# First layer's attention values: nine split products per chunk replaced by full-precision products on halves and quarters of the array

## Chip, cores and metric

The kernel runs on one core of a Trainium2 chip. The metric is the device time of one execution in microseconds (us). The kernel before takes 928.72 us, the median of 3 runs (927.98 to 929.9).

## The reference, cut to what matters

The network is two layers, each an attention onto a context of 154 keys per batch and a feed-forward part. The change touches only the attention of the first layer:

```
x: (2, 1024, 256)   ctx_768: (2, 154, 192)        all float32
q = (layernorm(x) @ Wq)  -> 16 heads of 64
k, v = ctx @ Wk, ctx @ Wv -> 16 heads of 64
attn = softmax(q @ k^T / 8) over the 154 keys of the same batch
x = x + tanh(g_xattn[0]) * ((attn @ v) @ Wo + bo)
```

After it come the first layer's mixture of 8 experts, a second attention (8 heads of 128, all 308 keys) and a coupling network. They are not changed.

## The kernel before

**Work and loops.** The 2048 rows of x are 16 tiles of 128. The attention goes through them two at a time: 8 pairs, in the function `pe_pairs` for TensorE and `dve_pairs`, `act_pairs`, `pool_first` for the other engines. The 16 heads lie in 8 chunks of 128 columns, two heads each; two chunks (four heads) are a group. A pair is worked off in 8 steps, n = 0 to 7. A "row" is what one step makes: the scores of one group (n // 2) for one of the two tiles (n % 2). The 8 pairs are peeled bodies and one hardware loop (pairs 5 and 6), which is the only place where pieces of the experts' weight W2 are split (L1046 on ScalarE in steps 1, 3 and 5, L827 on VectorE in steps 2, 4 and 6).

**Split products.** TensorE's fast float32r product is used with both operands split in a high and a low part, so one product is three matmuls (`pe_split`, L535 to L537). Plain f32 matmuls appear in the trace as two MATMUL records, each with a weight load of its own. The scores (L563) are plain f32: each head has a contraction of 64, and the two heads of a chunk lie on the upper and lower half of the array's rows and write two banks of the accumulator memory (PSUM).

**Order on TensorE.** The order is written out by hand. In step n: scores of row n + 1; transposes of row n - 1 (`pe_pair_probsT`, 5 transposes of 128x128, L573, into banks 4 and 5); a block of 12 split matmuls, which are queries in steps 0, 1, 6, 7 and output products in steps 2 to 5; then `values(n)`. In step 7 the transposes come before the scores. At the end of step 5 the next pair's x is transposed (L542) into bank 7, which must be free: it waits for `y_done`, the VectorE instruction (L834) that reads the output product of step 5 there. Bank 7 also holds the queries and outputs of all steps, so each block waits until the one before has been copied out.

**Values.** A chunk's values product (`pe_pair_pv`) takes three split products of 128x128 by 128x256 (both tiles at once): the 128 whole keys of either head, each with the other head's columns zero (`V0` has zero pads for it), and the remaining 26 keys of four heads, which lie at 32 partitions each in the fifth transposed block. That is 9 matmuls per chunk, 18 per group. The first chunk of a group runs at the end of an odd step, the second at the end of the even step that follows. Both write bank 6.

**The chain around it.** VectorE finds the row maximum (L877) of the scores. ScalarE does four exponentials with sums (L1084). VectorE takes reciprocals (L881), GpSimd multiplies (L1193, L1195) into the single buffer `normed`. After the transposes ScalarE copies them to the high part (L1066) and VectorE subtracts for the low part (L887). After a group's values ScalarE copies bank 6 to the high part of the output operand (L1071) and VectorE makes its low part (L894). ScalarE's and VectorE's queues are first in, first out. ScalarE's order in step n is: L1066 of row n - 1, the exponentials of row n + 1, a query copy (L1058, steps 0, 1, 6, 7) or x copy (L1053, step 5), in even steps L1071, and in the loop a piece of W2. VectorE's is: reciprocals of row n, row maximum of row n + 1, L887, normalising or statistics (L776), `add_y` (L834, steps 3 and 5), x low part (L869, step 5), in even steps L894, and in the loop a piece of W2.

**Before the first pair** the keys and values are computed (`pe_kv`, L427), 8 units for the values. ScalarE copies each to a high part (L474, L477) and VectorE subtracts (L456, L462).

Of the kernel before, what the change touches and what calls it, by code (L numbers as in the profile page):

```python
# [15 lines left out]
F32 = mybir.dt.float32  # L16
F32R = mybir.dt.float32r
U32 = mybir.dt.uint32
ALU = mybir.AluOpType
# [29 lines left out]
def flamingo(nc, t_in, out):  # L49
# [31 lines left out]
    with ExitStack() as ctx:  # L81
# [38 lines left out]
        def split_parts(offset, **shapes):  # L120
            with ExitStack() as place:
                if offset:
# [16 lines left out]
                                     for part in (W2_low, W2_high)]  # L139
        V0_WIDTH = 3 * 64 + P  # L140
        V0_high0, V0_low0 = split_parts(0, V0_high0=[P, NC, V0_WIDTH], V0_low0=[P, NC, V0_WIDTH])
        V0_high1, Wq0_high, xT0_low = split_parts(W2_SIZE, V0_high1=[P, NC, V0_WIDTH], Wq0_high=[P, DK, INNER],
                                                  xT0_low=[P, DK, PAIR])
# [3 lines left out]
        class Region:  # L147
# [20 lines left out]
        V0_low1, = split_parts(V0_AT, V0_low1=[P, NC, V0_WIDTH])  # L168
        P0_AT = V0_AT + NC * V0_WIDTH + 2 * 640 + NC * PAIR
        p0T_high, p0T_low, o0T_high = split_parts(P0_AT, p0T_high=[P, 2, 5, PAIR], p0T_low=[P, 2, 5, PAIR],  # L170
                                                  o0T_high=[P, NC, PAIR])
        V0 = ((V0_high0, V0_low0), (V0_high1, V0_low1))
# [11 lines left out]
        ctx_rows = reg_a.part(3 * DC, "p (r d) -> p r d", r=3)  # L184
        reg_a.at = P0_AT + 20 * PAIR
# [174 lines left out]
        o_ps = banks[:, 6, :]  # L360
        misc_ps = banks[:, 7, :]
# [6 lines left out]
        pT_parts = ((p0T_high, p0T_low), (pT_high, pT_low))  # L368
# [37 lines left out]

        def pe_kv(pe, units):
            pe.wait_ge(sem("wk_in0"), 16)
            for n in units:
# [4 lines left out]
                if n >= (4 if n < NC else NC + 3):  # L414
                    pe.wait_ge(sem("kv_sb"), n - (3 if n < NC else 2))
                    if n < NC:
                        pe.wait_ge(sem("kv_high"), n - 3)
# [28 lines left out]
        def dve_kv(dve, L, units):  # L446
            for n in units:
# [5 lines left out]
                elif kind == "v":  # L453
                    high, low = V0[a]
                    dve.wait_ge(sem("kv_high"), n + 1)
                    last = dve.tensor_tensor(whole_values(low, half), bank.rearrange("p (c i n) -> p c i n", c=4, i=2),  # L456
                                             whole_values(high, half).bitcast(F32), ALU.subtract)
                else:
                    high, low = V0[a]
                    dve.wait_ge(sem("kv_high"), n + 1)  # L460
                    for j in range(4):
                        last = dve.tensor_tensor(rest_values(low, half, j), rest_bank(bank, j),  # L462
                                                 rest_values(high, half, j).bitcast(F32), ALU.subtract)
# [1824 lines left out]
```

## Time and profile before

| | us |
|---|---|
| median of 3 runs (lowest, highest) | 928.72 (927.98, 929.9) |
| the profiled execution, device time | 927.16 |
| its span, first to last instruction | 925.3 |
| TensorE busy | 882.1 (95%) |
| VectorE busy | 563.1 (61%) |
| ScalarE busy | 519.3 (56%) |
| GpSimd busy | 373.7 (40%) |

PE is TensorE's matmuls, PEld its weight loads, DVE VectorE, ACT ScalarE, POOL GpSimd. Matmuls are pipelined: the duration of one is longer than the distance from its start to the next one's. A view that merges neighbours gives the start of the first and the length to the end of the last. The first layer's attention proper lies between about 42 and 300 us of the span.

### The profile page before, as it was taken

Reading aid. Unit: us, or ns where it says so; the run is one execution under the profiler, and the core shown is the slowest. Engines: PE = TensorE matmul, PEld = TensorE weight load, DVE = VectorE, ACT = ScalarE, POOL = GpSimd, SP = SyncE. Lnnn points to the kernel's source line nnn. Section 1 sums busy time; section 2 is a strip of 40 time slices with the busy share of each in tenths; the row PEclk is TensorE's granted clock in tenths of the full one; section 3 lists DMA queues with packets and bytes.
Section 4 is the critical chain, followed back from the end, with each engine's and each line's share of the span. In section 5 each row is a group of like instructions: output and inputs, shape, how many; then the busy total and the mean of one; then the engine's idle time right before and its main releaser. Section 6 shows DMA issues by size and latency. Waiting matters only on the chain.

```text
span 925.3 us, 20373 instructions
## 1 busy us (share of the span) xinstructions
PE 882.1 (95%) x6837; PEld 800.3 (86%) x6838; DVE 563.1 (61%) x1331; ACT 519.3 (56%) x1466; POOL 373.7 (40%) x530
## 2 busy tenths in 40 slices
PE   6989999999999999999999987999999999999996
PEld 4579999998898769999999986999999999987653
DVE  4665565556665774443444447877777776666466
ACT  5676776677775344334443462655655555552565
POOL 3173443444343143545455551534434443443000
PEclk9999999999999899999999997999999999999998
DMA  9000000330001557777777813000000000000002
GB/s 266 3 1 2 1 1 1 123 95 1 0 1 50 168 198 245 265 236 253 253 254 255 241 68 94 24 24 13 12 23 11 12 1 1 2 1 1 1 1 91
DMA packets 36674, 76.19 MB, mean 82 GB/s; under 512 B 4941, under 2 KB 22721, under 8 KB 36481
## 3 DMA queue, kind: packets, MB, share of 16 engines
q1 hardware_dynamic: 32865, 65.11, 21.8%
q0 software_dynamic: 3744, 10.23, 3.3%
q8 instruction: 39, 0.64, 0.3%
q14 instruction: 26, 0.21, 0.1%
HBM read 66.02 MB, written 9.31 MB: 81 GB/s over the span
## 4 chain that ended last, share of the span: by engine, by line
PE 87%; DVE 5%; DMA 3%; ACT 2%; issue 2%; POOL 1%; SPq 0%; DVEq 0%; POOLq 0%
PE banks L535 16%; PE banks L537 15%; PE banks L536 15%; PE banks L1530 14%; PE banks L573 8%; PE banks L563 5%; PE banks L427 3%; PE banks L1815 2%; PE banks L504 1%; PE banks L1826 1%; PE banks L1820 1%; PE banks L1808 1%; DMA region_a<-in_L_ffn_b 1%; PE banks L500 1%; PE banks L542 1%
## 5 line engine op out<-in xcount | busy, mean ns | idle before, releaser
L1084 ACT ACTIVATE region_a<-banks,negmax 128x154 f32<-128x154 f32 (+1 forms) x384 | 161.7, 434 | 29.1 <-DVE negmax L877 27.8
L1530 PE MATMUL banks<-region_b,region_a 128*128 128x128 f32 x1248 | 146.5, 276 | 1.2 <-ACT region_b L1566 1.2
L1530 PEld LDWEIGHTS banks<-region_b,region_a 128*128 128x128 f32 x1248 | 142.7, 192 | 2.1 <-ACT region_b L1566 0.9
L1230 POOL TENSOR_TENSOR region_a<-region_a,recip 128x640 f32<-128x640 f32 x64 | 80.3, 1255 | 136.1 <-DVE recip L881 136.1
L1193 POOL TENSOR_TENSOR region_a<-region_a,recip 128x512 f32<-128x512 f32 x64 | 66.7, 1042 | 138.6 <-DVE recip L881 99.5
L877 DVE TENSOR_REDUCE negmax<-banks 128x4 f32<-128x616 f32 (+1 forms) x128 | 100.5, 785 | 28.8 <-PE banks L563 15.5
L1621 DVE SCALAR_TENSOR_TENSOR region_b<-banks,region_a,region_b 128x128 f32<-128x128 f32 x156 | 43.9, 345 | 106.1 <-PE banks L1530 99.5
L573 PE MATMUL banks<-ident,region_a 128*128 128x128 f32 x640 | 94.0, 277 | 3.9 <-DVE pT_low L887 1.6
L573 PEld LDWEIGHTS banks<-ident,region_a 128*128 128x128 f32 x640 | 72.2, 140 | 14.1 <-issue 9.8
L535 PE MATMUL banks<-xT_high,Wq_high 128*128 128x256 f32 x256 | 78.3, 306 | 2.9 <-DVE xT_low L869 2.0
L1066 ACT CAST pT_high<-banks 128x640 fp32r<-128x640 f32 x64 | 44.4, 694 | 64.1 <-PE banks L573 64.1
L1084 ACT ACTIVATION_READ_ACCUMULATOR region_a<-banks,negmax 128x1 f32 x384 | 78.4, 204 | 0.0
L537 PE MATMUL banks<-xT_high,Wq_low 128*128 128x256 f32 x256 | 72.7, 284 | 0.0
L536 PE MATMUL banks<-xT_low,Wq_high 128*128 128x256 f32 x256 | 72.6, 284 | 0.0
L1066 ACT CAST p0T_high<-banks 128x640 fp32r<-128x640 f32 x64 | 44.6, 698 | 49.5 <-PE banks L573 49.5
L1573 ACT ACTIVATE region_b<-banks,region_a 128x128 f32<-128x128 f32 x156 | 44.6, 369 | 45.6 <-PE banks L1530 45.6
L887 DVE TENSOR_TENSOR p0T_low<-banks,p0T_high 128x640 fp32r<-128x640 f32 x64 | 52.6, 822 | 16.4 <-ACT p0T_high L1066 15.3
L887 DVE TENSOR_TENSOR pT_low<-banks,pT_high 128x640 fp32r<-128x640 f32 x64 | 52.7, 824 | 14.3 <-ACT pT_high L1066 13.1
L535 PE MATMUL banks<-p0T_high,V_high 128*128 128x256 f32 x192 | 54.9, 286 | 1.6 <-DVE o0T_low L894 1.6
L535 PEld LDWEIGHTS banks<-xT_high,Wq_high 128*128 128x128 f32 x256 | 49.0, 191 | 8.4 <-DVE xT_low L869 3.6
L535 PE MATMUL banks<-pT_high,V_high 128*128 128x256 f32 x192 | 54.3, 283 | 1.9 <-DVE oT_low L894 1.9
L1662 POOL COPY home_now<-home 128x1 uint32 (+1 forms) x39 | 20.7, 531 | 84.3 <-DVE region_b L1642 74.6
(294 smaller groups left out, 2542.2 us busy)
## 6 DMA issues: line engine op xcount, KB each, us to landing
region_a<-in_L_ffn_W SPq DMA_DIRECT2D x39, 1024.0 KB
W<-in_L_ffn_W SPq DMA_DIRECT2D x1, 4096.0 KB, 15.1
W<-y_rows SPq DMA_DIRECT2D x16, 256.0 KB, 2.8
out<-x SPq DMA_DIRECT2D x8, 256.0 KB, 2.2
x<-in_x SPq DMA_DIRECT2D x1, 1536.0 KB, 13.3
region_b<-in_L_xattn_Wq SPq DMA_DIRECT2D x1, 1024.0 KB, 9.4
region_b<-in_L_xattn_Wo SPq DMA_DIRECT2D x1, 1024.0 KB, 14.1
xn_rows<-region_b SPq DMA_DIRECT2D x1, 1024.0 KB, 4.8
```

The source lines that it names most:

```text
L535: pe.matmul(o, left[0], right[0], start=start, stop=False)
L536: pe.matmul(o, left[0], right[1], start=False, stop=False)
L537: return pe.matmul(o, left[1], right[0], start=False, stop=stop)
L563: mm = pe.matmul(scores[:, n % 2, i, u * NKEY:(u + 1) * NKEY], q0[half, c, rows], K0[half, b, c, 0:NKEY], start=True, stop=True)
L573: mm = pe.transpose(probsT_ps[:, m * P:(m + 1) * P], row[:, m * P:(m + 1) * P], ident[:])
L877: dve.tensor_reduce(into, source, AX.X, ALU.max, negate=True).then_inc(sem("bias_ready"), 1)
L887: dve.tensor_tensor(low[:, n // 2 % 2, :, at], probsT_ps[:, 0:640].rearrange("p (m n) -> p m n", m=5), high[:, n // 2 % 2, :, at].bitcast( ...
L1066: act.copy(pT_parts[L.index][0][:, n // 2 % 2, :, at], probsT_ps[:, 0:640].rearrange("p (m n) -> p m n", m=5))\
L1084: e = act.activation(into, source, ACT.Exp, bias=negmax[:, n % 2, u:u + 1], accum_out=sums[:, n % 2, u:u + 1])
L1193: pool.tensor_tensor(normed[:, 0:512].rearrange("p (j n) -> p j n", j=4), pr[:, :, 0:P], rc.broadcast_to([P, 4, P]), ALU.mult)
L1230: pool.tensor_tensor(probs1[:, n % 2], probs1[:, n % 2], rc, ALU.mult).then_inc(sem("p_norm"), 1)
L1530: mm = pe.matmul(banks[:, 2 * r + part, m * P:(m + 1) * P], W1[r][:, k, cols], xgT[:, r, k, :], start=(k == 0), stop=(k == DK - 1))
```

## The change

The values of a group are computed in one go, at the end of the even steps, and in plain f32, so neither the probabilities nor V nor their low parts are split. The whole keys of the two heads of a chunk go on the left and right half of the array's columns (128 rows by 64 columns each), without zero pads. The remaining keys of the four heads go on the four quarters (64 rows by 64 columns; within such a block the other head's rows hold zeros). The two chunks write two banks, 5 and 6, at columns 128 to 383, beside the fifth transposed block in bank 5.

```
+        p0T, o0T: f32 buffers;  V0 = (V0_first, V0_second), one buffer per batch in place of high and low
+        o0_ps = banks[:, 5:7, P:P + PAIR]

+        def pe_group_values(pe, g, b):
+            V = V0[b].bitcast(F32)
+            for u in range(2):
+                for i in range(2):
+                    pe.matmul(o0_ps[64 * i:64 * i + 64, u, :], V[:, 2 * g + u, 128 * i:128 * i + 64], p0T[:, g % 2, 2 * u + i, :],
+                              start=True, stop=False)
+            for i in range(2):
+                for u in range(2):
+                    rows = slice(64 * u, 64 * u + 64)
+                    mm = pe.matmul(o0_ps[64 * i:64 * i + 64, u, :], V[rows, 2 * g + u, 192 + 64 * i:256 + 64 * i],
+                                   p0T[rows, g % 2, 4, :], start=False, stop=True)
+            mm.then_inc(sem("o2_ps"), 1)

-        def pe_pair_probsT(pe, L, n):
+        def pe_pair_probsT(pe, L, n, groups_copied=None):
             for m in range(5):
+                if m == 4 and groups_copied is not None:
+                    pe.wait_ge(sem("o0_copied"), groups_copied)
                 mm = pe.transpose(probsT_ps[:, m * P:(m + 1) * P], row[:, m * P:(m + 1) * P], ident[:])
...
             for c in chunks:                                  # pe_pair_out
-                if c == NC - 2:
+                if L is L0 and r == 0 and c % 2 == 0:
+                    pe.wait_ge(sem("o2_sb"), groups_done - (NC - 2 - c) // 2)
+                if L is L1 and c == NC - 2:
...
+            probs_turned = "pt2_high" if L is L0 else "pt2_low"
                 def transposes(n):
-                            pe.wait_ge(sem("pt2_low"), s0 + s - 1)
-                        pe_pair_probsT(pe, L, (n - 1) % 8)
+                            pe.wait_ge(sem(probs_turned), s - 1)
+                        turned = L is L0 and n % 2 == 1 and not (first and n < 5)
+                        pe_pair_probsT(pe, L, (n - 1) % 8, 4 * i + n // 2 - 1 if turned else None)
                 def values(n):
+                    if L is L0:
+                        if n % 2 == 0 and not (first and n in (0, 2)):
+                            pe.wait_ge(sem(probs_turned), s)
+                            if not (first and n == 4):
+                                pe.wait_ge(sem("o0_copied"), group + n // 2 - 2)
+                            pe_group_values(pe, (n // 2 - 2) % 4, before if n < 3 else batch)
+                        return
...
             def probsT_rest(n, s):                            # VectorE
+                if L is L0:
+                    return
             def o_rest(g, group):                             # VectorE
+                if L is L0:
+                    dve.wait_ge(sem("o0_copied"), group + 1)
+                    dve.tensor_copy(high[:, part, :], o0T).then_inc(sem("o2_high"), 1)
                 dve.wait_ge(sem("o2_high"), g0 + group + 1)
-                dve.tensor_tensor(low[:, part, :], o_ps.rearrange("p (u n) -> p u n", u=2),
+                dve.tensor_tensor(low[:, part, :], o0T if L is L0 else o_ps.rearrange("p (u n) -> p u n", u=2),
...
             def o_high(g, group):                             # ScalarE
+                if L is L0:
+                    if not (isinstance(group, int) and group == 0):
+                        act.wait_ge(sem("o2_sb"), group)
+                    act.copy(o0T, o0_ps).then_inc(sem("o0_copied"), 1)
+                    return
```

So the transposed probabilities are copied once, by ScalarE, in f32. The group's output is copied once by ScalarE, to the f32 buffer `o0T`, and VectorE makes both the high part (a copy) and the low part (a subtraction) from it. In odd steps the fifth transpose waits for ScalarE's copy of the group's output, which lies in the same bank. Before the first pair the values are copied out of PSUM once each, by ScalarE and VectorE in turn (`copy_values`), and the zero fills of V shrink from eight to two. The tail after the last pair makes the same replacement for its last two groups.

## Rows read from the trace of the kernel before

**Rows 1.** The page: span, then the chain that ended last by engine

```profile
span 925.3 us, 20373 instructions
...
PE 87%; DVE 5%; DMA 3%; ACT 2%; issue 2%; POOL 1%; SPq 0%; DVEq 0%; POOLq 0%
```

**Rows 2.** Windows: one plain pair, one loop pair; length, engines' busy time, clock

```profile
123.36:155.58 32.22, 32.22 (x278) 29.51 (x277) 19.01 (x37) 22.69 (x81) 14.04 (x22) 1.00 0.01 2
...
220.52:253.25 32.73, 32.36 (x278) 29.52 (x277) 20.63 (x40) 24.23 (x84) 14.00 (x22) 1.00 0.00 0
```

**Rows 3.** Timeline of TensorE, end of step 0 to step 2: start, length, line

```profile
134.26 0.28 PE L535 MATMUL banks<-p0T_high,V_high 128*128 128x256 f32 x1
134.38 0.28 PE L536 MATMUL banks<-p0T_low,V_high 128*128 128x256 f32 x1
...
135.43 0.80 PE L563 MATMUL banks<-region_a 64*128 64x154 f32 x8
136.15 0.77 PE L573 MATMUL banks<-ident,region_a 128*128 128x128 f32 x5
136.67 0.37 PE L535 MATMUL banks<-xT_high,Wq_high 128*128 128x256 f32 x1
...
138.18 0.28 PE L535 MATMUL banks<-p0T_high,V_high 128*128 128x256 f32 x1
...
139.35 0.79 PE L563 MATMUL banks<-region_a 64*128 64x154 f32 x8
```

**Rows 4.** Timeline of TensorE in the coupling network: 512 columns, then 64-wide weights

```profile
874.92 1.45 PE L1815 MATMUL banks<-region_a,W 128*128 128x512 f32 x3
876.30 1.07 PE L1820 MATMUL banks<-region_a,W 128*64 128x512 f32 x2
```

**Rows 5.** Timeline of ScalarE, VectorE and GpSimd in step 1 (139.18: its query copy)

```profile
135.55 0.63 ACT L1071 CAST o0T_high<-banks 128x512 fp32r<-128x512 f32 x1
...
136.21 0.69 DVE L894 TENSOR_TENSOR o0T_low<-banks,o0T_high 128x512 fp32r<-128x512 f32 x1 [1.54 <-ACT o0T_high L1071]
...
136.90 0.77 DVE L877 TENSOR_REDUCE negmax<-banks 128x4 f32<-128x616 f32 x1
137.06 1.04 POOL L1193 TENSOR_TENSOR region_a<-region_a,recip 128x512 f32<-128x512 f32 x1 [2.52 <-DVE recip L881]
...
138.06 0.40 POOL L1195 TENSOR_TENSOR region_a<-region_a,recip 128x128 f32<-128x128 f32 x1
...
139.18 0.60 ACT L1058 COPY region_a<-banks 128x512 f32<-128x512 f32 x1
```

**Rows 6.** Groups of VectorE's instructions by line and shape: busy, mean ns

```profile
L827 DVE TENSOR_TENSOR W_low<-W,W_high 128x512 fp32r<-128x512 f32 x10 | 6.2, 687 | 0.0
...
L462 DVE TENSOR_TENSOR V_low<-banks,V_high 32x128 fp32r<-32x128 f32 x16 | 4.6, 287 | 2.0 <-ACT V_high L477 1.8
...
L1955 DVE COPY W<-W 64x128 f32<-64x128 f32 x1 | 0.2, 210 | 0.0
```

**Rows 7.** Timeline, steps 6 and 7: ScalarE's output copy and TensorE around it

```profile
127.44 0.71 PE L573 MATMUL banks<-ident,region_a 128*128 128x128 f32 x5
...
127.64 0.59 ACT L1071 CAST o0T_high<-banks 128x512 fp32r<-128x512 f32 x1
...
128.07 0.80 PE L563 MATMUL banks<-region_a 64*128 64x154 f32 x8
```

**Rows 8.** Timeline, end of step 5: last values, statistics, output sum, x transposes

```profile
153.89 0.28 PE L535 MATMUL banks<-p0T_high,V_high 128*128 128x256 f32 x1
...
154.13 0.42 DVE L776 BATCH_NORM_STATS2 loop_stats<-x 128x6 f32<-128x256 f32 x1
154.47 0.47 DVE L834 SCALAR_TENSOR_TENSOR x<-banks,gates,x_biased 128x256 f32<-128x256 f32 x1
...
154.99 0.33 PE L542 MATMUL banks<-ident,xn 128*128 128x128 f32 x1
```

**Rows 9.** Timeline of VectorE in a loop pair: a piece of W2

```profile
209.05 0.68 DVE L827 TENSOR_TENSOR W_low<-W,W_high  x1
```

More of the change, by code:

```diff
@@ L184, in flamingo @@
         ctx_rows = reg_a.part(3 * DC, "p (r d) -> p r d", r=3)
+        reg_a.at = P0_AT
+        p0T = reg_a.part(10 * PAIR, "p (q m n) -> p q m n", q=2, m=5)
+        reg_a.at += 3 * DC
+        o0T = reg_a.part(2 * PAIR, "p (u n) -> p u n", u=2)
+        assert reg_a.at <= P0_AT + 20 * PAIR
         reg_a.at = P0_AT + 20 * PAIR
@@ L405, in kv_bank, with values_by, values_count, copy_values @@
             return banks[:, n % 4] if n < NC else banks[:, 4 + (n - NC) % 3]
+        def values_by(n):
+            return "kv_high" if (n - NC) % 2 == 0 else "kv_sb"
+        def values_count(n):
+            return NC + (n - NC) // 2 + 1
+        def copy_values(copy, n):
+            kind, b, half = kv_units()[n]
+            bank, into = kv_bank(n), V0[b].bitcast(F32)
+            if kind == "v":
+                return copy(whole_values(into, half), bank.rearrange("p (c i n) -> p c i n", c=4, i=2))
+            for j in range(4):
+                last = copy(rest_values(into, half, j), rest_bank(bank, j))
+            return last
         def pe_kv(pe, units):
@@ L452, in dve_kv @@
                     last = dve.tensor_scalar_mul(head_keys(a, 0), keys_of(bank, 0), L.scale)
[L453 to L457, printed above, removed]
-                else:
[L459 to L463, printed above, removed]
+                elif values_by(n) == "kv_sb":
+                    dve.wait_ge(sem("kv_ps"), n + 1)
+                    dve.wait_ge(sem("v_pads"), 1)
+                    last = copy_values(dve.tensor_copy, n)
+                else:
+                    continue
                 last.then_inc(sem("kv_sb"), 1)
@@ L469, in act_kv @@
                 bank = kv_bank(n)
+                if kind != "k" and values_by(n) != "kv_high":
+                    continue
                 act.wait_ge(sem("kv_ps"), n + 1)
@@ L472, in act_kv @@
                     last = act.activation(head_keys(a, 1), keys_of(bank, 1), ACT.Copy, scale=L.scale)
-                elif kind == "v":
-                    last = act.copy(whole_values(V0[a][0], half), bank.rearrange("p (c i n) -> p c i n", c=4, i=2))
-                else:
-                    for j in range(4):
-                        last = act.copy(rest_values(V0[a][0], half, j), rest_bank(bank, j))
+                else:
+                    last = copy_values(act.copy, n)
                 last.then_inc(sem("kv_high"), 1)
@@ L758, in pe_pairs @@
                 pe_rows(pe, 3)
-            pe.wait_ge(sem("pt2_low"), s0 + STEPS)
-            pe.wait_ge(sem("o2_sb"), g0 + GROUPS - 1)
-            for u in range(2):
-                pe_pair_pv(pe, L, 3, u, b)
+            pe.wait_ge(sem(probs_turned), STEPS)
+            if L is L0:
+                pe.wait_ge(sem("o0_copied"), GROUPS - 1)
+                pe_group_values(pe, 3, b)
+            else:
+                pe.wait_ge(sem("o2_sb"), g0 + GROUPS - 1)
+                for u in range(2):
+                    pe_pair_pv(pe, L, 3, u, b)
             if L is L1:
@@ L1090, in first_layer @@
                 zero = zero_eps[:, 0:1]
-                for high, low in V0:
-                    for part in (high, low):
-                        act.copy(part[:, :, 64:128], zero.unsqueeze(2).broadcast_to([P, NC, 64]))
-                        z = act.copy(part[:, :, 192:320], zero.unsqueeze(2).broadcast_to([P, NC, P]))
+                for part in V0:
+                    z = act.copy(part.bitcast(F32)[:, :, 192:320], zero.unsqueeze(2).broadcast_to([P, NC, P]))
                 z.then_inc(sem("v_pads"), 1)
```

61 lines of the change are left out of this document (28 added, 33 removed).

## The prediction

> **What bounds the kernel now.** I read the page first: a span of 925.3 us, with 87% of the chain that ended last on TensorE [rows 1]. Which part of that the change can touch, the windows tell: in a pair of the first layer's attention TensorE's busy time is the whole length, 32.22 of 32.22 us, at a granted clock of 1.00, while VectorE has 19.01, ScalarE 22.69 and GpSimd 14.04 [rows 2]. So TensorE bounds each pair, and each matmul less there is worth its distance to the next. But the other three are not idle by much more than a third, and they are a chain with TensorE. The timeline shows how much room that chain has: in step 1 the query copy ends at 139.78 [rows 5], and TensorE would need it (bank 7) at the block of step 2, 1.25 us after 139.35, that is at 140.60 [rows 3]. The room is 0.8 us. The loop pairs, with pieces of W2, take 32.73, 0.5 more [rows 2]: there the chain already shows.
>
> **The matmuls.** A split matmul of 256 columns takes 0.12 us to the next one [rows 3], so the 18 of a group are 2.16. An f32 record takes, at 512 columns, (1.45 - 0.59) / 2 = 0.43 us to the next, 0.59 being the length of a last one (1.07 less the 0.48 between the two starts of 64-wide weights) [rows 4]; for 256 columns I take half, 0.215. Each f32 matmul is two records. Eight records of 154 columns would need 8 x 0.13 = 1.03 one after the other at that rate per column; the scores' eight are over in 0.80 with their last one's tail [rows 3]: records on the two halves of the rows run at the same time. If halves of the columns do the same, and quarters too, the whole keys take 2 chunks x 2 records = 4 slots and the remaining keys 2 slots: 6 x 0.215 = 1.29. That is the value I take; its other end (no overlap between column halves) is a rival below.
>
> **Change of array shape.** From the last 128-wide record (874.92 + 2 x 0.43 = 875.78) to the first 64-wide one (876.30) is 0.52 against 0.43, and between the two 64-wide ones it is 0.48 [rows 4]: 0.09 + 0.05 = 0.14 for a change (its ends: nothing, if the loads are pulled ahead, and 0.2, if both sides of a change cost what this one does on top). The group adds two changes (into column halves, into quarters); the one into the scores' shape was there before: +0.28. In step 7 transposes follow, so a third is added: 0.13. Per group 2.16 - 1.29 - 0.28 = 0.59 less, say 0.58; per pair 2.32 - 0.13 = 2.19. If this were all, eight pairs would give 17 us.
>
> **The chain behind the group.** What goes: VectorE's low part of the probabilities (L887), one subtraction per row. In the plain pairs it ran beside TensorE's work, so it buys nothing by itself; what is late next is the copy and the output, below. What comes: VectorE now makes two passes over a group's output, and VectorE's queue has the row maximum behind them, ScalarE's the exponentials behind that, and the query copy behind those. And an odd step no longer has values in it: it shrinks from 3.92 (135.43 to 139.35) by 9 x 0.12 to 2.84, while the chain starts where it did, at the end of the group.
> The added pass is an f32 copy of 512 columns, which the trace doesn't show. A copy of 128 columns took 0.21, a subtraction of 128 0.29, of 512 0.69 [rows 6]. The subtractions give 0.154 fixed and 1.04 ns per column; with the same fixed part the copy has 0.44 ns per column, so 0.38 for 512. The ends are 0.21 and 0.69; I take 0.40, near the copy's own row.
> Count from the start of the odd step's scores. ScalarE's output copy starts at 0.12 [rows 3, 5] and takes 0.60; VectorE starts at 0.76, copy to 1.16, low part (0.69, as L827 from on-chip memory [rows 6]) to 1.85, row maximum 0.77 to 2.62. From there ScalarE's next copy starts 1.51 later (137.67 to 139.18 [rows 5]), at 4.13, and ends at 4.73. TensorE can go on 0.05 later, as after L834 (154.94 to 154.99 [rows 8]), at 4.78.
>
> **The new waits, per pair.** (a) Step 7: the transposes come right after the group, and the fifth waits for the output copy: 0.72 + 0.05 = 0.77 instead of 0.44, so 0.33. Their distance to the scores was 0.63 [rows 7] and becomes 0.97. (b) Step 0: block ready at 0.97 + 0.73 + 1.51 + 0.09 + 1.25 = 4.55, allowed at 4.78: 0.23. (c) Step 2: block ready at 2.84 + 1.25 = 4.09, allowed at 4.78: 0.69. (d) Step 5: the values stood between the output block and the x transposes, 1.10 us (153.89 to 154.99), and hid the output sum (L834) [rows 8]. Now the block's last matmul starts at 2.64, is readable 0.33 later (134.26 + 8 x 0.12 = 135.22 to the output copy's 135.55 [rows 3, 5]), the sum takes 0.47, and its 0.42 of statistics before it end at 3.04 too: done at 3.5, against 2.76: 0.76. In the other odd steps the fifth transpose comes at 0.72 + 0.44 = 1.16, after the copy; nothing there. The sum is 2.01 against 2.19 gained: a plain pair goes from 32.22 to 32.04.
>
> **Loop pairs.** A piece of W2 takes 0.68 on VectorE, 0.62 to the next start, and stands between the low part and the row maximum [rows 9]. It adds 0.62 to (b) and to (d). In step 4 it makes a wait: reciprocals of the row end at 1.85 + 0.62 + 0.17 = 2.64, GpSimd's two products 1.04 and 0.40 [rows 5] at 4.1, the transposes were ready at 2.84 + 0.72 = 3.56: 0.55. Together 1.8, where before paid 0.5: 33.84 against 32.73, so 1.1 slower each.
>
> **First and last pair.** The values' production is bounded by its matmuls; only the last unit's low parts (four of 0.29 [rows 6]) leave its end, and the first pair is paced by GpSimd, which also splits Wo there. I take -0.3, between -1.2 and +0.5. In the last pair (d) is gone, no x follows, but normalised rows enter VectorE's chain: 2.2 - 1.25 - some of that gives -0.6, between -1.2 and +0.8. The tail loses one low part and gets two passes and a wait: 0.
>
> **Sum.** Pairs 1 to 4: -0.7. Pairs 5 and 6: +2.2. First and last: -0.9. Total +0.6 on the profiled execution's 927.16, so 927.8. The median of the runs shown lies 1.56 above that execution; against it I forecast **929.3**, no change that can be told (0.2% is 1.9 us, and that is my bound).
>
> **A rule against it.** In the rows, two halves of the array's rows cost no more than one [rows 3]. The Trainium skill ("TensorE: Matmul & The Clock Gate", section "Measured speedup vs the span model") gives 2.38x for three column tiles, not 3x. As an estimate from that figure a slot of column halves could take up to 1.26 x 0.215, so 0.22 more per group and 7 us in all, 936. No row of this trace has two column halves at once.
>
> **Rivals.** (1) The halves of the columns don't overlap: the change doesn't do what it says. For it: the only 64-wide matmuls here (L1820) run singly, and two column halves need two full 128-row streams of f32 at once, while the two score products shared one stream's width. Against it: the row halves overlap fully. Price: 4 slots more, 0.86 per group; above 0.58 it makes every group slower. The new waits stay, since they start at the group's end. Over some 30 of the 32 groups (the first pair has room) 26 us: 955, slower. (2) The chain is shorter than I count: if the two passes or the exponentials keep their room, waits (b) and (c) vanish, and half of (d). For it: ScalarE has 9.5 us of idle time in a pair. Then 1.3 per pair more, and in loop pairs another 1: 917 to 925, 919 the middle. With no wait at all it is 913. (3) The copy of 512 columns runs at the subtraction's rate, 0.69: +0.29 in (b), (c), (d) and later (step 4 too), 0.9 to 1.1 per pair: 937. For it: it also rounds to another type. Against: the copy's row.
>
> **How the numbers follow.** The forecast has 0.40, within 925 to 934; rival 1 0.14 (948 to 957), rival 2 0.24 (913 to 925), rival 3 0.16 (933 to 940), and 0.06 for others, of both signs. The range 917 to 946 leaves out rival 1 (0.13), the lower part of rival 2 (0.05) and a little of the rest. Faster by over 0.2%: 0.23 from rival 2 and 0.12 from the forecast's lower part, 0.35. Slower: 0.14 + 0.16 + 0.12 + 0.03 = 0.45. Within: 0.20, nearly all from the forecast.
>
> **What would show it.** Right: six slots of about 0.215 per group, with pairs of records that start together; a group from first to last start in 1.3 us; TensorE idle before the step 2 block on ScalarE's query copy (0.7), before the x transposes on L834 (0.8), at the fifth transpose of step 7 on the output copy (0.3); plain pairs near 32.0 and loop pairs near 33.8. Wrong: eight or more slots for the whole keys (rival 1), a pair near 30 (rival 2), a copy well over 0.4 (rival 3). An added wait in other steps, or a pair whose TensorE has no idle time and is still not shorter, would mean that the matmul or switch cost is mis-sized.

## The result and the profile after

The changed kernel takes **935.7 us** (median of 8 runs, 932.32 to 940.58); the kernel before took 928.94 beside it (8 runs, 924.39 to 932.29). The ratio is 1.0077, 95% interval 1.0054 to 1.0100. In a second session, with more runs of both, it was 933.62 against 927.45, ratio 1.0061 (1.0039 to 1.0083). So the change costs 6 to 7 us, where I had forecast none. The profiled execution of after took 937.22 us.

First the page of the kernel after: span, busy times, and the chain that ended last by engine.

```profile
span 935.5 us, 20231 instructions
...
PE 878.3 (94%) x6773; PEld 757.8 (81%) x6774; DVE 523.7 (56%) x1289; ACT 511.4 (55%) x1450; POOL 373.3 (40%) x530
...
PE 80%; DVE 7%; ACT 5%; issue 3%; DMA 3%; POOL 1%; DVEq 0%; SPq 0%; ACTq 0%; POOLq 0%
```

TensorE's share of the chain falls from 87% [rows 1] to 80%, and what it loses goes to VectorE and ScalarE. Matmul work was removed, and waits on the chain stand in its place.

The windows of after: the plain pair and the two loop pairs, each from one set of x transposes to the next, then the tail, from the first transposes of the router's rows to the first matmul behind its logits. Columns: window, length, then busy time (instructions) of PE, PEld, DVE, ACT, POOL, the granted clock as a share of 2.4 GHz, DMA share, GB/s.

```profile
121.86:154.09 32.23, 31.04 (x268) 23.78 (x269) 14.44 (x33) 22.70 (x83) 14.04 (x23) 1.00 0.01 2
186.32:219.93 33.61, 31.18 (x269) 23.79 (x269) 15.72 (x35) 23.57 (x85) 14.09 (x23) 1.00 0.19 53
219.93:254.12 34.19, 31.27 (x269) 23.78 (x269) 16.31 (x36) 23.97 (x86) 14.01 (x23) 1.00 0.00 1
288.14:318.24 30.10, 27.49 (x204) 21.97 (x203) 16.55 (x78) 13.05 (x30) 8.58 (x15) 0.87 0.31 97
```

The same tail in the kernel before:

```profile
286.27:312.17 25.90, 24.05 (x202) 22.91 (x200) 16.45 (x77) 12.73 (x28) 8.51 (x14) 1.00 0.37 113
```

Against [rows 2] the plain pair has nearly the old length, but 1.2 us of it is now idle TensorE (the view counts the end of a last matmul as busy; from start to start the waits are 2.1, below). The loop pairs are 0.9 and 1.5 longer. The tail is 4.2 us longer, and its mean clock is 0.87 where it was 1.00: stretches of it run at 1.2 GHz, half the upper level of 2.4. Length times clock is 26.2 against 25.9, so nearly all of the 4.2 us goes with the clock.

TensorE around one group of values in after, with ScalarE and VectorE behind it (start, length, engine, line; idle time before it in brackets). It answers to [rows 3, 5].

```profile
133.61 1.08 PE L598 MATMUL banks<-region_a,V_first 128*64 128x256 f32 x8
134.62 0.66 PE L603 MATMUL banks<-region_a,V_first 64*64 64x256 f32 x8
135.22 0.79 PE L578 MATMUL banks<-region_a 64*128 64x154 f32 x8
135.35 0.58 ACT L1121 COPY region_a<-banks 128x512 f32<-128x512 f32 x1 [0.62 <-PE banks L603]
135.94 0.76 PE L590 MATMUL banks<-ident,region_a 128*128 128x128 f32 x5
135.97 0.43 DVE L939 CAST o0T_high<-region_a 128x512 fp32r<-128x512 f32 x1 [3.46 <-ACT region_a L1121]
136.43 0.69 DVE L941 TENSOR_TENSOR o0T_low<-region_a,o0T_high 128x512 fp32r<-128x512 f32 x1
...
137.13 0.77 DVE L920 TENSOR_REDUCE negmax<-banks 128x4 f32<-128x616 f32 x1
...
139.40 0.59 ACT L1105 COPY region_a<-banks 128x512 f32<-128x512 f32 x1
...
140.05 0.39 PE L550 MATMUL banks<-Wo_high,o0T_high 128*128 128x256 f32 x1 [0.50 <-ACT region_a L1105]
```

Sixteen records of values fit into 1.61 us, from 133.61 to 135.22. Eight on column halves take 1.01 and eight on quarters 0.60. In the trace the two records of a pair of halves, and the four of the quarters, start 6 to 7 ns apart, and the next ones follow 0.215 us later (0.267 for the first behind a change of shape): the halves and the quarters run side by side. Behind them one sees the chain of the prediction, link by link: output copy, high copy, low rest, row maximum, and at the end TensorE before the output block of step 2, waiting for ScalarE's query copy.

The end of step 5 in after, which answers to [rows 8]:

```profile
153.19 0.42 DVE L819 BATCH_NORM_STATS2 loop_stats<-x 128x6 f32<-128x256 f32 x1
153.23 0.28 PE L552 MATMUL banks<-Wo_high,o0T_low 128*128 128x256 f32 x1
...
153.55 0.48 DVE L877 SCALAR_TENSOR_TENSOR x<-banks,gates,x_biased 128x256 f32<-128x256 f32 x1
...
154.09 0.33 PE L557 MATMUL banks<-ident,xn 128*128 128x128 f32 x1 [0.58 <-DVE x L877]
```

And TensorE in step 7, which answers to [rows 7]: the fifth transpose waits for the output copy, and the scores start 1.03 behind the first instead of 0.63.

```profile
127.16 1.10 PE L590 MATMUL banks<-ident,region_a 128*128 128x128 f32 x5
128.19 0.79 PE L578 MATMUL banks<-region_a 64*128 64x154 f32 x8
```

The tail of after on TensorE: the last row's transposes wait 1.34 us for GpSimd, and the third group's values behind them, at 1.2 GHz, take 1.98 and 1.13 us instead of 1.08 and 0.66.

```profile
294.91 0.76 PE L590 MATMUL banks<-ident,region_a 128*128 128x128 f32 x5 [1.34 <-POOL region_a L1245]
297.08 1.98 PE L598 MATMUL banks<-region_a,V_second 128*64 128x256 f32 x8
298.99 1.13 PE L603 MATMUL banks<-region_a,V_second 64*64 64x256 f32 x8
```

### The profile page after: what moved, and what is told of

Read it like the earlier page. It is cut to its first block, busy times and chain, and to the rows that moved or that the text cites. A ratio compares the mean times of both kernels' runs of the same rounds, so it can differ in the third digit from the quotient of the medians.

```text
span 935.5 us, 20231 instructions
## 1 busy us (share of the span) xinstructions
PE 878.3 (94%) x6773; PEld 757.8 (81%) x6774; DVE 523.7 (56%) x1289; ACT 511.4 (55%) x1450; POOL 373.3 (40%) x530
## 4 chain that ended last, share of the span: by engine, by line
PE 80%; DVE 7%; ACT 5%; issue 3%; DMA 3%; POOL 1%; DVEq 0%; SPq 0%; ACTq 0%; POOLq 0%
PE banks L1580 14%; PE banks L550 13%; PE banks L552 12%; PE banks L551 12%; PE banks L590 6%; PE banks L598 4%; PE banks L448 3%; PE banks L1865 2%; PE banks L578 2%; ACT region_a L1136 2%; PE banks L603 2%; ACT region_a L1121 2%; DVE negmax L920 1%; PE banks L519 1%; PE banks L1876 1%
## 5 line engine op out<-in xcount | busy, mean ns | idle before, releaser
L590 PE MATMUL banks<-ident,region_a 128*128 128x128 f32 x640 | 96.2, 279 | 7.8 <-POOL region_a L1245 5.3
L939 DVE CAST o0T_high<-region_a 128x512 fp32r<-128x512 f32 x32 | 13.7, 427 | 105.6 <-ACT region_a L1121 105.6
L1113 ACT COPY region_a<-banks 128x640 f32<-128x640 f32 x64 | 44.8, 700 | 28.5 <-PE banks L590 27.3
L552 PE MATMUL banks<-pT_high,V_low 128*128 128x256 f32 x192 | 54.0, 281 | 0.0
```

Source lines behind the costliest of these rows:

```text
L552: return pe.matmul(o, left[1], right[0], start=False, stop=stop)
L590: mm = pe.transpose(probsT_ps[:, m * P:(m + 1) * P], row[:, m * P:(m + 1) * P], ident[:])
L1113: act.copy((p0T if L is L0 else pT_high)[:, n // 2 % 2, :, at], probsT_ps[:, 0:640].rearrange("p (m n) -> p m n", m=5))\
```

## The experiments

My theory: TensorE's saving is real and is spent on waits for one chain, the two passes over a group's output that stand ahead of the row maximum on VectorE's queue. The rival: the new matmuls, or their new place, cost more than I counted, and the chain is harmless.

Besides the time I read each run's mean granted clock. The product of span and clock, run by run, is a coarse measure of the work: what the execution would have taken at the full clock, if TensorE bounded all of it. It corrects too much, since among 32 runs of the kernel before 0.01 of clock went with 5.5 us, not 9.3 (with 8.2 among the 23 of session 3). The standard error of a product is 0.2 to 0.7 us. The edits are shown shortened, partly in words. Means over the runs:

```
kernel                 runs  span us  clock   clock x span
before (session 1)      18   925.8    0.9861  912.9
a1_changed_again         7   932.0    0.9833  916.4
e1_placement_alone       6   943.0    0.9817  925.7
e2_max_before_rest      12   926.2    0.9862  913.4
e3_copy_twice            6   941.2    0.9835  925.6
before (session 2)      32   926.9    0.9869  914.8
e4_w2_behind_max        11   932.7    0.9813  915.3
e5_sum_before_stats     12   927.8    0.9830  912.0
e6_values_in_tail_gap   10   931.5    0.9852  917.7
e7_all_reordered        12   928.8    0.9848  914.6
before (session 3)      23   926.4    0.9871  914.5
e10_sum_first_alone      6   932.5    0.9845  918.0
e8_order_and_tail       12   926.6    0.9854  913.1
e9_fill_first_pair      12   928.9    0.9852  915.2
before (session 4)      17   925.9    0.9859  912.8
e11_step5_copy_early    12   925.9    0.9838  910.9
```

### a1: the changed kernel again

> The changed kernel once more, beside the kernel before on the same chip, as the reference for the three others. Theory: slower by 0.5 to 1.0% (5 to 9 us). The profile shows whether what comes on top of the pairs (tail of the first attention, drops of TensorE's clock there and in the experts) is the same in a second execution: if it is a matter of the clock's chance alone, the tail is within 0.5 us of the one before and the drops are elsewhere.

933.62 us, ratio 1.0061. Of the 6.2 us between the spans the clock accounts for 1.5 to 2.6 (0.0028 at 5.5 to 9.3 us per 0.01), the rest, 3.6 to 4.7, is work and waits. The pairs are those of the first trace to 0.4 us. The tail is 29.32, 0.8 under it. The clock is at half at 53 and 295 us as there (at 51 and 297), the second time for 6.8 us instead of 3.4; what was 10.2 us from 314 is 3.4 from 319. So the places come again, the lengths don't.

### e1: the placement alone

```diff
 # kernel before, values(n) of the first layer
-  odd step: chunk 0 of the group; next even step: chunk 1
+  even step: wait o2_sb; chunks 0 and 1 of the group (split matmuls)
```

> The kernel before with its own split matmuls, but both chunks of a group at the end of the even step, as the change places them. Theory (placement and the chain behind it eat the saving): odd steps are 2.84 us, and waits of 0.2 (step 0), 0.3 (step 2) and 1.1 (step 5, the low part of the probabilities is before the output sum) appear, 1.6 per pair; 12 to 16 us slower than before, about 942. Rival (the saving in matmuls isn't there, placement is free): within 2 us of before, 927 to 931.

944.52 us, ratio 1.0181 (1.0151 to 1.0211). One plain and one loop pair of e1:

```profile
126.60:160.40 33.80, 32.86 (x277) 29.58 (x277) 18.68 (x37) 22.77 (x81) 13.96 (x22) 1.00 0.01 1
228.71:263.85 35.14, 33.16 (x277) 29.61 (x277) 20.39 (x40) 24.01 (x85) 13.93 (x22) 1.00 0.00 0
```

With the old matmuls and only the new place a plain pair is 1.58 longer than in [rows 2]. So the place costs this much. The rest of the change (the cheaper matmuls, VectorE's subtraction less and its copy more) gives it back in plain pairs: 33.80 to 32.23. The waits of e1 are the expected ones: 0.2 in step 0, 0.24 in step 2, 1.1 in step 5.

### e2: the row maximum ahead of the output passes

```diff
+ LATE_REST = (1, 5, 7)
  in step n of these: reciprocals(n); row_max(n + 1)
+ then o_rest of the group that step n - 1 would have worked off
```

> The changed kernel, but in steps 1, 5 and 7 VectorE takes the row maximum before the two passes over the group's output, not after. Theory: the waits before the query blocks of steps 0 and 2 vanish (0.2 + 0.74 per pair), those at step 7's fifth transpose (0.4) and before the x transposes (0.77) stay; plain pairs 31.3 us, loop pairs about 32 (the pieces of W2 no longer stand before the maximum); 9 us less than the changed kernel, about 926. Rival (another engine or the passes themselves bound the pair): 932 to 936.

927.77 us, ratio 0.9999 (0.9980 to 1.0017). With one change of order on VectorE the median is that of the kernel before. But look where:

```profile
122.69:155.02 32.33, 30.84 (x269) 23.75 (x269) 16.35 (x33) 22.74 (x81) 16.07 (x23) 1.00 0.01 2
220.46:253.52 33.06, 30.99 (x268) 23.77 (x269) 18.96 (x36) 24.05 (x84) 16.95 (x23) 1.00 0.00 1
```

The loop pairs fell to 33.07, the last body from 34.0 to 32.75, but the plain pairs rose by 0.1 where I had expected 31.3, and VectorE and GpSimd are each 2 us busier with the same instructions. All eight pairs are 2.1 shorter than a1's (270.09 for 272.19), still 0.8 over before (269.29). That is less than half of the 5.8 us between the mean spans of a1 and e2. The product with the clock has 3.0 of them; the rest goes with a mean clock higher by 0.0029, which no run explains.

Of the waits, (c) fell from 0.74 to 0.16 (now for GpSimd, ahead of step 2's transposes). (b) stayed at 0.20: from the scores of step 7 to the query block it is 3.80 us in after, in e1 and in e2, so the row maximum, the exponentials and the query copy take that long by themselves. (d) grew by 0.70. The timeline of step 5 in e2 says why:

```profile
152.46 1.24 POOL L1247 TENSOR_TENSOR region_a<-region_a,recip 128x512 f32<-128x512 f32 x1 [2.96 <-PE banks L590]
152.83 1.41 DVE L943 TENSOR_TENSOR o0T_low<-region_a,o0T_high 128x512 fp32r<-128x512 f32 x1
153.66 0.84 POOL L1249 TENSOR_TENSOR region_a<-region_a,recip 128x128 f32<-128x128 f32 x1
```

Moved behind the row maximum, the low rest falls on GpSimd's two products, and all three slow each other: 1.41 for 0.69, 1.24 and 0.84 for 1.04 and 0.40. Of the 24 low rests between 91 and 285 us in e2, the 12 with these products beside them took 1.41, six with nothing of GpSimd beside them 0.69, and six beside other work of GpSimd 1.11. In the changed kernel all 24 took 0.69. The Trainium skill ("SBUF — State Buffer", section "Who interferes with whom") states that a VectorE instruction with two inputs from on-chip memory contends with a GpSimd instruction that reads it, since the second input comes by a shared port. The trace agrees, with these numbers. The low rest of before read one input from PSUM; by that rule it was outside this contention.

### e3: the copy twice

```diff
+ dve.tensor_copy(o0T_spare, o0T)
  dve.tensor_copy(high[:, part, :], o0T).then_inc(sem("o2_high"), 1)
```

> The changed kernel with the copy to the high part made twice (the first into a buffer that nobody reads), 0.43 us more on VectorE per group. Theory (VectorE's passes are on the chain): three waits per pair grow by 0.43, plain pairs 33.5, in all 10 to 13 us more than the changed kernel, about 947. Rival (the chain has slack and the matmuls bound it): less than 3 us more.

942.30 us, ratio 1.0161 (1.0133 to 1.0189), 8.7 over a1: less than the theory's sum, far more than the rival's. Plain pair 33.56, loop pairs 34.98 and 35.52.

```profile
L940 DVE COPY region_a<-region_a 128x512 f32<-128x512 f32 x32 | 13.7, 427 | 106.2 <-ACT region_a L1123 106.2
```

A copy of 0.43 us more makes a plain pair 1.33 longer, three times its length, on an engine that is busy 16 us of 34. The theory had three places that pay 0.43 each; the trace has four that pay about 0.3: (b), (c), (d), and one in the output block of step 4, where the weight load waits for the low part itself:

```profile
149.05 0.19 PEld L551 LDWEIGHTS banks<-Wo_high,o0T_high 128*128 128x128 f32 x1 [0.30 <-DVE o0T_low L943]
```

### e4: W2's pieces behind the row maximum too

```diff
  on e2, loop pairs:
- W2_rest at the end of steps 2, 4, 6
+ W2_rest behind the row maximum of steps 3, 5, 7
```

> e2_max_before_rest with one more thing moved: in the two loop pairs before the last the VectorE piece of W2 (0.4 us or so each) stands behind the next row maximum (steps 3, 5, 7) instead of at the end of steps 2, 4, 6. e2's loop pairs last 33.07 us against 32.36 of its plain pairs. Theory (the row maximum is late behind whatever stands ahead of it on VectorE, W2's pieces as much as the output copy): the loop pairs fall by 0.3 to 0.7 each, the median to about 926.8. Rival (the loop pairs' excess is ScalarE's W2 copies, 0.6 us each in steps 1, 3, 5, not VectorE's): loop pairs stay at 33.0 to 33.1, the median at 927.8.

933.79 us, ratio 1.0053 (1.0032 to 1.0074): both theory and rival wrong. The loop pairs became longer, 33.72 and 35.03 (the second, like the last body, with half clock in this trace); e7 against e8 shows the edit cleanly, 33.40 and 33.38 against 32.76 and 32.74. That is 1.3 us of the median; more of it goes with the clock, the lowest mean of all sets (0.9813). The piece is no longer ahead of the row maximum, but ahead of the output sum for which the x transposes wait (the longest such wait is 2.2 us in e4, 1.4 in e2). It went from one place of the path to another.

### e5: the output sum ahead of the statistics

```diff
  on e2, step 5:
- stats_of(previous tile); add_y
+ add_y; stats_of(previous tile)         (in step 7 the statistics move too)
```

> e2_max_before_rest with VectorE's output sum of step 5 put ahead of the statistics of the tile before (0.42 us) instead of behind them. It tests wait (d) of the prediction, which e2 shows at up to 1.4 us before the x transposes (1.2 in the changed kernel). Theory (the chain high copy, low rest, statistics, output sum ends that wait, so every piece taken out of it comes off the pair): plain pairs fall from 32.36 to about 31.95, median about 925. Rival (the wait is ended by the last output matmuls or by POOL's biased tile and VectorE's queue is only as late as these): plain pairs stay at 32.3 to 32.4, median 927.8.

The pairs did as the theory said, 32.36 to 32.00, loop pairs 32.73. The profiled execution was 2.9 us ahead of the kernel before at the first transposes of rows (283.33 against 286.27), and the median stayed: 928.36, ratio 1.0012 (0.9983 to 1.0040). Against the kernel before the product with the clock is lower by 2.9 us, the clock by 0.0039. The tail of e5, with TensorE's order of the changed kernel, has full clock throughout:

```profile
283.33:308.98 25.65, 24.00 (x204) 19.61 (x203) 16.77 (x79) 12.96 (x28) 9.00 (x15) 1.00 0.38 114
```

It isn't longer than before's 25.90. (Its wait for GpSimd is 0.39 instead of 1.34, since the row maxima come earlier.)

### e6: the third group's values in the tail's gap

```diff
  behind the last pair:
+ pe_group_values(2)          (ScalarE: o_high(2) first)
  pe_pair_probsT(7)
  pe_logits(1); pe_rows(2)
- pe_group_values(2)
```

> The changed kernel with one edit behind the last pair: the values of the third group and ScalarE's copy of them stand ahead of the last row's probability transposes, where TensorE waits 1.35 us for POOL, instead of behind the logits and rows that follow. Theory (the idle stretch from 290 to 296 us is what lets the granted clock fall to half there, which the kernel before, busy throughout, does not do): PEclk between 292 and 302 stays at 1.00, and the stretch from the first transposes of rows to the output matmuls becomes 15.91 minus about 1.3 of idle and minus about 1.5 of half clock, 13 us; the median falls from 933.6 to 931 or a little under. Rival (the clock falls there anyway, by the load since the start): a drop of the same 3.4 us comes at 295 to 305, only the idle time is saved, 932.4 or more.

933.13 us, ratio 1.0056 (1.0037 to 1.0076). The windows of e6, a plain pair and the tail:

```profile
123.04:155.27 32.23, 31.04 (x268) 23.77 (x268) 14.45 (x33) 22.70 (x83) 14.05 (x23) 1.00 0.01 2
289.33:317.54 28.21, 26.25 (x205) 21.63 (x203) 16.59 (x78) 13.06 (x30) 8.59 (x15) 0.92 0.34 103
```

The fall of the clock at 297 is gone, and the tail is 1.1 to 1.9 shorter than in the two traces of the changed kernel (29.32, 30.10); but at 313 the clock falls as in these (314, 319). The wait for GpSimd is 0.12 instead of 1.34, and a new one of 0.67 comes behind it, for ScalarE's copy (L1337) ahead of the router's logits. Length times clock is 26.0, against 25.8 and 26.2: what the tail gains goes with the clock. That the edit keeps the clock up is not shown either. e7 and e11 have the same edit and fall to half at 297 and 295; e5 doesn't have it and doesn't fall. The median is in e6's session no better than a1's in its own, which was the rival's forecast.

### e7: all three edits

> All three together on the changed kernel: VectorE's output copy and W2 pieces behind the row maximum, the output sum ahead of the statistics, the third group's values in the gap behind the last pair. Theory (the four waits that the change made are matters of order on VectorE's queue, and their parts add up): 927.8 less 1, 2.5 and 2.5, about 922, under the kernel before by 0.6%. Rival (TensorE's queue is then bound by the next wait of the chain, POOL's probabilities, and the gains overlap): 925 to 927, no difference from before.

930.60 us, ratio 1.0016 (0.9998 to 1.0033). Above the range of theory and rival both; e4's edit, which costs 0.65 in each loop pair, is 1.3 of it. The clock falls at 297 with the gap filled:

```profile
295.00:300.00 5.00, 4.33 (x29) 2.39 (x28) 0.00 (x0) 1.17 (x2) 0.55 (x1) 0.72 0.13 43
```

### e10: the output sum first, alone

```diff
  on the changed kernel, step 5:
- stats_of(previous tile); add_y
+ add_y; stats_of(previous tile)
```

> The changed kernel with only the output sum of step 5 put ahead of the statistics (the output copy stays where the change put it). In e5_sum_before_stats both edits were made, and its plain pairs fell from 32.36 to 32.00 us. Theory (wait (d) is VectorE's queue, and each edit acts by itself): plain pairs 32.23 less 0.42, 31.81, loop pairs 33.60 and 34.19 by as much less; granted clock times span, 916.4 in a1, becomes about 914; median 931. Rival (the sum only then waits for the output matmuls): plain pairs stay at 32.23, median 933.6.

933.52 us, ratio 1.0071 (1.0046 to 1.0096); plain pairs 32.27, loop pairs 33.31 and 34.20, so only the first of these gained. The rival is right. With nothing ahead of it the sum waits for the last output matmul:

```profile
154.13 0.48 DVE L877 SCALAR_TENSOR_TENSOR x<-banks,gates,x_biased 128x256 f32<-128x256 f32 x1 [0.27 <-PE banks L552]
```

In after (above) the statistics, 153.19 to 153.61, only fill that time. In e5 they mattered because the slow low rest had pushed everything back. So wait (d) has a floor, set by TensorE itself: the sum's own 0.48 and the way there and back.

### e8: e5 with the tail edit

> e5_sum_before_stats with the third group's values in the gap behind the last pair, and W2's pieces left where they were. e5's spans times their granted clock give 911.96 us against 914.82 of the kernel before on the same chip, but its mean clock was 0.9830 against 0.9869, and the two cancelled. Theory (two terms: work, and what the clock grants): clock times span 911 to 912, since e5 hadn't any half clock in the tail; the median then follows the mean clock, 926 at 0.985. Rival (the tail edit is worth 1.3 us of work, as its gap was long): clock times span 910.5, median 925.

927.79 us, ratio 1.0000 (0.9977 to 1.0023); plain pair 32.03, loop pairs 32.76 and 32.74, and the tail, at full clock:

```profile
285.10:311.40 26.30, 24.24 (x204) 19.61 (x203) 16.77 (x79) 12.97 (x28) 9.00 (x15) 1.00 0.37 111
```

Clock times span is 913.1, over both forecasts (911 to 912, and 910.5). At full clock the tail edit makes the tail 0.65 longer than e5's, not shorter.

### e9: matmuls in the gaps of the first pair

```diff
+ for _ in range(6): pe.matmul(o0_ps[:, 1, 0:P], ident, ident)
  transposes(n)                       # first pair, n = 2, 3, 4
```

> e8_order_and_tail with 18 more matmuls (the identity by itself, 128 columns, into the values' second bank, six each ahead of the probability transposes of steps 2, 3 and 4 of the first pair), where TensorE waits for POOL 0.9 us a step. They compute nothing that is used. Four of the traces of the changed kernel and its variants have 3.4 us of half clock at 51 to 55 us, the kernel before has none there. Theory (it is these idle gaps that let the clock fall): no half clock between 48 and 58, mean clock 0.001 to 0.002 above e8's, median 1 us under e8's. Rival (the clock's falls aren't set by these gaps): half clock at 51 to 55 or the same mean clock as e8, median equal to e8's or up to 1 us above it by the added matmuls.

929.95 us, ratio 1.0031 (1.0007 to 1.0054). The mean clock is e8's, and e8 itself, with the gaps open, had full clock there in its trace: the rival holds for the clock. The time is 2.2 us over e8's, more than the rival's 1: the first pair, 40.43 for 38.20, has all of it, so the added matmuls weren't free in the gaps. One look at a clock that falls is no proof of what made it fall.

### e11: step 5's passes early, those of 1 and 7 late

```diff
  on e8:
- LATE_REST = (1, 5, 7)
+ LATE_REST = (1, 7)
```

> e8_order_and_tail with the output copy and low rest of step 5's group back at the end of step 4, ahead of the row maximum, and those of steps 1 and 7 still behind it. In e8's trace the low rest (both inputs in on-chip memory) lasts 0.69 us where GpSimd computes nothing, and 1.41 where GpSimd's two products of the row run beside it, as in step 5, ahead of the output sum for which the x transposes wait. Theory (that overlap is what limits e8's pairs: the low rest's end at 154.39 pushes the output sum): step 5's low rest returns to 0.69, GpSimd's products of that step from 1.24 and 0.84 to 1.04 and 0.40, and the wait before the x transposes from up to 1.0 to 0.5 to 0.6 us, plain pairs 31.5 to 31.7. Rival (the row maximum of step 5 is then 1.1 us later again, and ScalarE's exponentials and the query blocks of steps 6 and 7 inherit it, as in the changed kernel): plain pairs 32.0 or longer, a new wait on ScalarE's copies in step 6 or 7.

The windows of e11 (plain pair, loop pair, tail), then its timeline at the end of step 5:

```profile
121.20:152.83 31.63, 30.85 (x268) 23.76 (x268) 15.60 (x34) 22.69 (x83) 15.41 (x23) 1.00 0.01 2
217.08:249.98 32.90, 31.01 (x268) 23.79 (x269) 17.73 (x37) 24.02 (x85) 15.86 (x23) 1.00 0.00 1
283.12:315.73 32.61, 30.56 (x204) 25.04 (x203) 16.93 (x79) 13.05 (x30) 8.98 (x15) 0.78 0.29 89
```

```profile
150.55 0.69 DVE L944 TENSOR_TENSOR o0T_low<-region_a,o0T_high 128x512 fp32r<-128x512 f32 x1
...
151.41 1.04 POOL L1250 TENSOR_TENSOR region_a<-region_a,recip 128x512 f32<-128x512 f32 x1 [3.41 <-DVE recip L927]
...
152.29 0.48 DVE L878 SCALAR_TENSOR_TENSOR x<-banks,gates,x_biased 128x256 f32<-128x256 f32 x1 [0.27 <-PE banks L552]
152.41 0.40 POOL L1252 TENSOR_TENSOR region_a<-region_a,recip 128x128 f32<-128x128 f32 x1
```

The theory holds: the low rest is back at 0.69, GpSimd's products at 1.04 and 0.40, the plain pairs at 31.63, the shortest of all kernels here and 0.6 under [rows 2]. (The two loop pairs together are as long as e8's, 65.5.) The waits that end in (d) fell as far as the output matmuls allow: 3.5 us in all between 91 and 280 us, where e8 had 5.9. And again the median is 928.11, ratio 0.9998 (0.9979 to 1.0017). This trace had the clock at half from 295 to 305 and from 312 to 322, and a tail of 32.61 us.

## Why the prediction was right or wrong

The differences from before, part by part (us; the profiles of after and a1, 935.5 and 930.8 against 925.3):

```
                                            forecast   after     a1
up to the first x transposes                   0       -1.33   +0.26
first pair                                    -0.3     -0.60   -0.56
next four pairs                               -0.7     +1.04   +0.68
two loop pairs                                +2.2     +2.35   +2.34
last body                                     -0.6     +0.41   +0.44
tail                                           0       +4.20   +3.42
from there to the experts' part                0       -1.36   -1.97
all behind, where no code changed              0       +5.49   +0.89
sum                                           +0.6    +10.20   +5.50
```

**The matmuls: right.** Six slots, full overlap. A group takes 1.61 us where I had 1.29 + 0.28 = 1.57 and went on with 1.58. The estimate from the Trainium skill's figure ("TensorE: Matmul & The Clock Gate", section "Measured speedup vs the span model"), 0.22 more per group, isn't borne out: 1.01 us for the four slots of column halves, where four of 0.215 and one change of shape are 1.00. That its 936, and the 937 of rival 3, lie next to the measured 935.7 is chance: neither mechanism is there.

**The copy: right in size.** 0.427 us against 0.40; rival 3 (0.69) is out.

**The four waits: right in size.** (a) 0.40 for 0.33, (b) 0.20 for 0.23 (the query block at 131.99 instead of 131.79), (c) 0.74 for 0.69 (140.05 instead of 139.31), (d) 0.77 for 0.76: 2.11 for 2.01. e3 shows that VectorE's queue is on the path: a copy more costs 1.33 us a plain pair. For (b) the two passes aren't needed: they end as the scores become readable, and e1 and e2 have the same 0.20. (d) has a floor in TensorE's own output matmuls (e10). Plain pair: 32.23 for 32.04. The 0.19 are 0.10 in the waits and about 0.1 in four groups of 0.03.

**Loop pairs: right.** 33.60 and 34.19 for 33.84 each, together 2.3 over before for 2.2.

**Pairs 1 to 4 and the last: a step that failed.** "Pairs 1 to 4: -0.7" took four plain pairs. Three of them stayed as they were; the one from 55.39 to 89.62 is 1.0 longer (a1: 0.7): TensorE is idle in it for 3.1 us against 0.8 before (1.2 in the plain pairs of after), the longest time, 1.3, for VectorE's low part of x near its start. The last body is 0.4 slower for 0.6 faster: I let (d) go, but TensorE is idle there for 1.55 us and was not before, 0.54 and 0.50 of it for ScalarE's query copies (L1105), the longest ones. Together these are 2.7 us of the miss (a1: 2.4).

**The first pair: right in sign, too small.** It is 0.6 faster for 0.3, but with 3.4 us at half clock. e4 has the same TensorE order there and full clock, and takes 38.20, 2.1 under before.

**The tail and the clock: the other step that failed.** "The tail loses one low part and gets two passes and a wait: 0." It is 4.2 longer in the profile of after and 3.4 in a1's. Where the wait comes I had missed: in the kernel before half a group's split matmuls stood between the last rows' transposes and covered the wait for GpSimd's last products; now a group's values come only behind both its rows, and the wait of 1.34 is bare. But the matmuls that went make up for it. At full clock the tail is no longer than it was: length times clock is 26.2 (after) and 25.8 (a1) against 25.9, and e5's and e8's tails, with full clock, take 25.65 and 26.30. What is longer is the time that TensorE spends at 1.2 GHz: 8.0 us of the tail in after, 6.8 in a1, none before. Of the 4.2 and 3.4 us, 1.4 and 2.0 come back by the start of the experts' part (26.56 and 25.95 against 27.92).

So the term that failed there is one that the sum didn't have: the granted clock, taken as before's. It is 0.980 against 0.988 in the profiled executions, half-clock time 2 x 0.020 x 935.5 = 37 us against 22, and over the runs of a1's session 31 against 26. It makes 1.5 to 2.6 of the 6.2 us there. Of the 10.2 us between the two profiles 5.5 lie in code that didn't change, 0.9 in a1's, so the one profile of after says little of what the change costs.

What sets the clock is **open**. The better orders don't get their gain in time: e5 and e11 have less work than before by 2.9 and 1.9 us (clock times span) and the same time, at a clock lower by 0.004 and 0.002. Filling the gaps of the first pair doesn't raise the mean clock (e9). Filling the gap of the tail went with one fall less in e6, and not in e7 and e11. All sets but e2's (0.9862) have a lower mean clock than the kernel before beside them, e1's too, which has the old matmuls and only waits more. More than this the runs don't show.

The range held the time, and the case that I had held likeliest was the right mechanism in the plain and the loop pairs; but the sign came out slower, for two bodies that I took for plain ones and for a clock that I had put at before's.

## What to carry to other kernels

A cheaper product isn't a cheaper step if its results come later and in one lump: count what the old product covered where it stood, body by body. On a queue shared by several chains the order is worth as much as the work: one line's move (the row maximum ahead of the output passes) took 3 us of work and waits out of this change, and one pass more is paid in every place where the queue is late. Length times clock tells which part of a longer stretch is work: here it turned a tail 4 us longer into one of the old length. Before moving an instruction on VectorE look at what it then runs beside: with two inputs in on-chip memory it lasted twice as long beside GpSimd's.

## What the hardware showed that I had not expected

- Records on two column halves, with 128 rows and 256 columns of f32 each, started 6 to 7 ns apart and shared one slot of 0.215 us, and those on four quarters likewise (1.01 us for eight records on halves, 0.60 for eight on quarters, changes of shape included).
- One stretch of 3.4 us at 1.2 GHz in the first pair goes with 1.5 us more: 39.73 in e2, 38.20 in e4, whose code is the same there.
- The contention of VectorE's subtraction with GpSimd's products: 0.69 to 1.41 us, and 0.40 to 0.84 for the small product.
- Three orders whose eight pairs are 2.7 to 2.8 us shorter in the trace from the first x transposes to the first of the router's rows (e5, e8, e11: 266.5 to 266.6 against 269.3), moved no median: ratios 1.0012, 1.0000 and 0.9998, each at a mean clock under that of the kernel before beside it.
